# Items of 244 rows in a routed AdaLN block: fewer moving columns per product, a reordered bridge into the expert loop, a loop with a running item number

## What is computed

```python
mod = (_silu(L0_c) @ L0_wmod).reshape(4, 6, 1, -1)            # sa, ca, ga, sb, cb, gb
h = _layernorm(x) * (1 + ca) + sa
q, k, v = heads(h @ Wq.T), heads(h @ Wk.T), heads(h @ Wv.T)
q, k = _rms_norm(q), _rms_norm(k)                             # per head, width 16
y = softmax(q @ k.T * 16 ** -0.5) @ v
vn = v / norm(v)
x = x + ga * ((y - sum(y * vn) * vn) @ Wo.T)
h = _layernorm(x) * (1 + cb) + sb                             # 2048 rows
probs = softmax(h @ router_w.T)
w = _top_p_weights(probs, 0.9)                                # 2048 x 8, zero where not kept
for e in range(8):
    out += ((silu(h @ gate_w[e].T) * (h @ up_w[e].T)) @ down_w[e].T) * w[:, e:e + 1]
x = x + gb * out
```

## Time and profile before

| | |
|---|---|
| median of 3 runs | 493.86 us |
| the profiled execution | 491.9 us |
| its span, first to last instruction | 490.3 us |
| TensorE busy | 457.1 us, 93% |
| VectorE / ScalarE / GpSimd busy | 334.5 / 258.9 / 199.1 us |
| mean granted TensorE clock | 0.986 |

### The profile page before, as it was taken

How to read it: one execution, slowest core, us unless ns; L and a number is a source line. 1 busy time by engine, 2 the same in 40 slices (tenths; PEclk the granted TensorE clock), 3 DMA queues, 4 the chain that set the end, 5 groups by cost and what they waited for, 6 DMA issues and landing times. The chain is left out here.

```text
span 490.3 us, 10014 instructions
## 1 busy us (share of the span) xinstructions
PE 457.1 (93%) x3466; PEld 349.2 (71%) x3466; DVE 334.5 (68%) x790; ACT 258.9 (53%) x358; POOL 199.1 (41%) x235
## 2 busy tenths in 40 slices
PE   7978989998999999999999799999989999999992
PEld 7373343454535445345899799989979999999992
DVE  3597786499767976768898768557437585665542
ACT  3237878767776788677452245344226353524230
POOL 4142033013100200004235667566756666676755
PEclk8899999999999999999999899999999999999998
DMA  8601203901010100223334547757537556565443
GB/s 258 225 1 45 87 2 30 128 16 43 2 45 1 44 1 11 79 87 111 109 127 114 128 92 171 198 111 192 89 68 177 131 128 158 117 119 111 78 77 45
DMA packets 30785, 46.01 MB, mean 94 GB/s; under 512 B 3588, under 2 KB 22276, under 8 KB 30728
## 3 DMA queue, kind: packets, MB, share of 16 engines
q0 software_dynamic: 11936, 22.50, 25.9%
q1 hardware_dynamic: 18792, 22.77, 14.1%
HBM read 34.44 MB, written 12.93 MB: 97 GB/s over the span
## 5 line engine op out<-in xcount | busy, mean ns | idle before, releaser
L645 ACT ACTIVATE probs<-psS 128x1024 f32<-128x1024 f32 x128 | 123.1, 1028 | 21.4 <-PE psS L1487 21.1
L1730 PE MATMUL psS<-hs_hi,w_hi 128*128 128x256 f32 x400 | 113.1, 283 | 3.0 <-issue 2.3
L1730 PE MATMUL psS<-hs_lo,w_hi 128*128 128x256 f32 x400 | 112.4, 281 | 0.0
L1730 PE MATMUL psS<-hs_hi,w_lo 128*128 128x256 f32 x400 | 112.3, 281 | 0.0
L506 POOL DMA_INDIRECT out<-y_sel,idx_out x44 | 76.7, 1744 | 35.8 <-DVE y_sel L1293 22.7
L1730 PEld LDWEIGHTS psS<-hs_hi,w_hi 128*128 128x128 f32 x400 | 75.3, 188 | 4.1 <-issue 4.1
L1730 PEld LDWEIGHTS psS<-hs_lo,w_hi 128*128 128x128 f32 x400 | 75.3, 188 | 0.0
L1730 PEld LDWEIGHTS psS<-hs_hi,w_lo 128*128 128x128 f32 x400 | 75.3, 188 | 0.0
L492 POOL DMA_INDIRECT h_sel<-h_rows,idx_in x50 | 55.8, 1115 | 43.7 <-DVE sel L1259 19.3
L1594 PE MATMUL psY<-probs,v_aug 128*32 128x512 f32 x512 | 68.2, 605 | 0.0
L697 ACT ACTIVATE silu_g<-psS 128x512 f32<-128x512 f32 x50 | 29.8, 598 | 59.2 <-PE psS L1730 58.8
(11 more groups left out here) (224 smaller groups left out, 736.7 us busy)
## 6 DMA issues: line engine op xcount, KB each, us to landing
w_in<-gateT SPq DMA_DIRECT2D x8, 512.0 KB, 4.8
w_in<-upT SPq DMA_DIRECT2D x8, 512.0 KB, 4.5
w_in<-downT SPq DMA_DIRECT2D x8, 512.0 KB, 4.7
h_rows<-h_nat SPq DMA_DIRECT2D x4, 528.0 KB, 3.1
x_all<-x SPq DMA_DIRECT2D x4, 512.0 KB, 5.2
h_rows<-mod_table POOLq DMA_DIRECT2D x4, 512.0 KB, 15.0
out<-x_all SPq DMA_DIRECT2D x4, 512.0 KB, 2.9
mod_rows<-mod_table SPq DMA_DIRECT2D x3, 512.0 KB, 5.7
```

Source lines behind the costliest of these rows:

```text
L645: act.activation(probs[:, gk % 4, 2 * pair:2 * pair + 2, :], psS[:, pair, :, :], ACT.Exp, scale=ATT_SCALE).then_inc(probs_done, 1)
L1730: mm = pe.matmul(ps[:, i * SW:(i + 1) * SW], w, v[:, k, :], start=at == 0, stop=at == 3 * KC - 1)
```

## The change

- **244 rows.** An item has SW = 2 x PR rows, PR = 122. TSLOTS (tiles of an expert) becomes 18 instead of 16. Gather, scatter, transposes, `sel` and `output` work on 122 partitions; `gate_up` moves 244 columns, `downs` has 122 stationary columns and still moves 256. Tile and row of a place come from a multiplication, a rounding by adding and subtracting 1.5 * 2^23, and one fused step, all in float32, in place of shift, mask and two casts.
- **Full last items.** Since 9 items of 244 hold more than 2048 rows, code for a ninth item of an expert (`clear_places`, `replace_places`) is added behind a comparison; it runs only where an expert has nine items.
- **Bridge.** On VectorE `take_weights(3)` goes ahead of `product(2, 0)`; the second list's `rows_of_places(1)`, `count_items` and the tiles of experts 2 to 7 go later; on ScalarE `gate(3, 0)` goes between the two `round_hidden(2, ...)`; on TensorE `list_tokens(1)` goes behind the first half of `downs(2)`.
- **Loop.** The loop for a fourth and later item counts a register `item` up; it makes six turns, and for four items the body stands in the fourth.
- **Early lists.** `list_early(0)` is summed ahead of the value matmuls of step 11 and copied by itself, `list_early(1)` behind them; `turn(0)` goes from step 15 to step 14; `turn_h` of step 6 goes behind that step's value matmuls.
- **Roots.** One Newton step of three instructions and one step of higher order in four; its factor 0.375 is applied where the root is used.
- **Start and v.** The twelve `kT` matmuls and two copies are gone, `stay_awake(18)` is `stay_awake(30)`; the parts of the first two tiles of sequence 0 are copied by ScalarE, those of the other two by GpSimd as before; the copy to `v_aug` is made by ScalarE for all sequences.

```diff
+    PR = 122
+    TSLOTS = S * -(-T // (S * PR))
-    SW = S * P
+    SW = S * PR
...
+                    turns = end - a
+                    with eng.register() as item:
+                        eng.reg_mov(item, before + a)
+                        with eng.Fori(0, turns) as i:
+                            with eng.If(n > (i + turns - 3) % turns + a):
+                                m = eng.snap(item, min_val=EARLY + a, max_val=EARLY + ITEMS)
...
+                                body(e, False, m)
+                                eng.reg_add(item, item, 1)
...
-                    pool.indirect_dma_start(h_sel[:, k, :], None, h_rows[0:rows, :],
-                                            bass.IndirectOffsetOnAxis(ap=idx_in[:, k:k + 1], axis=0)).then_inc(gathered, 16)
+                    pool.indirect_dma_start(h_sel[0:PR, k, :], None, h_rows[0:rows, :],
+                                            bass.IndirectOffsetOnAxis(ap=idx_in[0:PR, k:k + 1], axis=0)).then_inc(gathered, 16)
...
+            for tt in range(2):
+                q, k = parted[:, tt, 0:H, :, :], parted[:, tt, H:HG, :, :]
+                act.wait_ge(lo_done, tt + 1 + 1)
+                act.copy(q[:, :, 1:3, :], q[:, :, 0:4:3, :]).then_inc(parts0_done, 1)
+                act.copy(k[:, :, 1, :], k[:, :, 3, :]).then_inc(parts0_done, 1)
+                act.copy(k[:, :, 2, :], k[:, :, 0, :]).then_inc(parts0_done, 1)
+            take_v(0, range(TT))
...
+                dve.tensor_tensor(t, y, y, ALU.mult).then_inc(newton_step, 1)
+                dve.tensor_tensor(t, t, z, ALU.mult).then_inc(newton_step, 1)
+                dve.scalar_tensor_tensor(out=t, in0=t, scalar=-10.0 / 3.0, in1=t, op0=ALU.add, op1=ALU.mult).then_inc(newton_step, 1)
+                dve.scalar_tensor_tensor(out=y, in0=t, scalar=5.0, in1=y, op0=ALU.add, op1=ALU.mult).then_inc(newton_step, 1)
...
-            stay_awake(18)
-
-            pe.wait_ge(awake_in, 2)
-            for cols in (P, 2 * P - 12, 2 * P):
-                for _ in range(4):
-                    pe.matmul(psS[:, 1, 1, 0:cols], kT[:, 1, 0, 0:P], kT[:, 1, 0, 0:cols], start=True, stop=True)
+            stay_awake(30)
...
-                    tok = slice(j * P, (j + 1) * P)
+                    tok = slice(j * PR, (j + 1) * PR)
...
-                list_tokens(1)
                 pe.wait_ge(w_ready, 6)
                 downs(2, 1, js=(0,))
+                list_tokens(1)
                 turn(4)
```

More of the change, by code:

```diff
@@ L58, in adaln_block @@
     RING = 4
-    SW = S * P
+    SW = S * PR
+    ROUND = 1.5 * 2.0 ** 23
     GATE_ROW, SHIFT_ROW, SCALE_ROW = 0, B, 2 * B
@@ L282, in item_counts, with last_item, walk_items @@
             return n, before
-        def walk_items(eng, body, between):
+        def last_item(e):
+            return (T - (SLOTS0 * PR if e < EXPERTS0 else 0)) // SW
+        def walk_items(eng, body, between, fullest=None):
             for e in range(E):
@@ L290, in others @@
                         with eng.If(n > i):
+                            if fullest:
+                                with eng.If(i > last_item(e) - 1):
+                                    fullest(e, before + i)
                             body(e, False, before + i)
@@ L295, in last_others @@
                     end = TSLOTS // S
[L296 to L299, removed]
+                    turns = end - a
[4 more added lines that the diff above has]
+                                m = eng.snap(item, min_val=EARLY + a, max_val=EARLY + ITEMS)
+                                if fullest:
+                                    with eng.If(m - before > last_item(e) - 1):
+                                        fullest(e, m)
+                                body(e, False, m)
+                                eng.reg_add(item, item, 1)
                 body(e, True, before)
@@ L442, in double_parts @@
                 pool.tensor_copy(k[:, :, 2, :], k[:, :, 0, :]).then_inc(parts_done, 1)
-            for tt in range(TT):
+            for tt in (2, 3):
                 double_parts(0, tt)
@@ L985, in take_logits @@
                                 psM[:, 1, 0:TT * E].rearrange("p (t e) -> p t e", e=E)).then_inc(logit_done, 1)
-            dve.wait_ge(ident_done, 1)
-            for half in range(2):
-                dve.tensor_copy(kT[:, 1, 0, half * P:(half + 1) * P], ident[:, :]).then_inc(awake_in, 1)
             dve.wait_ge(x0_in, 16)
@@ L1289, in output @@
                 for k in range(S):
-                    row = sel[:, bass.ds(m % RING, 1), k, :].rearrange("p a c -> p (a c)")
+                    row = sel[0:PR, bass.ds(m % RING, 1), k, :].rearrange("p a c -> p (a c)")
                     if last:
                         dve.wait_ge(last_ps, k + 1)
-                    weighed = dve.scalar_tensor_tensor(out=into[:, k, :], in0=down_rows(k, last),
+                    weighed = dve.scalar_tensor_tensor(out=into[0:PR, k, :], in0=down_rows(k, last),
                                                        scalar=row[:, bass.ds(e1, 1)], in1=row[:, 1 + E:], op0=ALU.mult, op1=ALU.mult)
```

213 lines of the change are left out of this document (131 added, 82 removed).

## The result

The changed kernel takes 679.57 us (median of 4 runs, 678.44 to 680.16), the kernel before 493.11 us (4 runs): a ratio of 1.3853, 95% interval 1.3807 to 1.3898. The ratios with intervals come from executions in the faster of the chip's two states alone, and differ a little from the quotient of the medians, here 1.378. I had forecast 478.5 us.

A forecast was written before the change was run, and what follows sets the result against it. TensorE, busy 457.1 of 490.3 us, was taken as the bound. Columns -7.0, bridge -3.4, loop -0.2, start -1.1, attention -1.5, last sequence -1.2 sum to -14.4: 477.5 from 491.9, given as 478.5 us, range 471.5 to 485.5.

The forecast's parts named there:

- column term: Gate and up products: 244 columns save 6.5 ns on each of 1200 matmuls, 7.8 us, less 0.8 in gather waits: -7.0.
- the gathers take the place of the columns: Rival: the chain turn, sel, gather, turn sets an item's pace, all 7.8 us become waits for h_sel, 485.5 us; chance 0.13.
- signs of being wrong: 244 columns at 118 ns, `downs` at another distance, 26 or more items, or TensorE's h_sel waits above 4 us in sum.
- Start, attention, last sequence: Before the items: cheaper roots and shared copies -1.1 at the start, -1.5 in attention; reordered last sequence -1.2 us.
- Bridge: Before item 4: the 2.56 us gather wait and low clock go, first product at 275.3 instead of 278.70: -3.4 us.
- What I called late next: Bridge: `count_items`, now between `product(3, 1)` and `split_input(4)`, with ScalarE's list copy and `round_input(4)` behind it.
- The reason given for the long gather(4): Bridge: its first instruction took 3.58 us, not 1.04, beside `w_lo` and two `a_lo`, instructions with two SBUF inputs.
- gather(5) under the big tile instructions: Bridge: by the skill's rule this gather would be long, about 2.5 us back; the prediction relied on the rows instead.
- Loop: Expert 3's fourth item: the 2.30 us issue wait falls to about 1.1, about 1.0 comes behind it: -0.2 us.
- Short stationary operands: Rival: loads of 122 columns in `downs` take twice a matmul's distance, 71 us added: 549 us; chance 0.03.

The follow-up runs named there:

- e2: Kernel before, only the gathers of items 1 and later over 122 rows instead of 128, scatters at 128: 604.39 us, ratio 1.2333.
- e3: Kernel before, only the scatters over 122 rows instead of 128, gathers at 128: 671.42 us, ratio 1.3701.
- e9: Changed kernel whole, but gathers (except the first, of 128) and scatters carry 120 rows instead of 122: 481.95 us against 490.29, ratio 0.9831.
- e10: e9 with the two moves of e8: 482.56 us, ratio 0.9841.
- e1: Changed kernel with PR = 128 (256-row items, DMAs of 128 rows), every other part kept: 486.01 us against 490.8, ratio 0.9914.
- e11: Kernel before, gate and up products moving 244 of 256 columns, nothing else: 487.93 us against 490.29, ratio 0.9932.
- e4: e1 with gate and up products moving only 244 of 256 columns: 483.93 us, ratio 0.9874.
- e8: e1 with two moves: ScalarE's round_input(4) before the counts' wait and list copy, VectorE's count_items before product(3, 1): 484.29 us against 492.08, ratio 0.9845.
- e6: Kernel with the old bridge order and 120 rows in each DMA: as quick as 128 rows, 4188 small packets; its time is not in the text.
- e7: Kernel with the old bridge order and 112 rows in each DMA: time a little above the expected 485 to 493 us.

## Why the prediction was wrong

**The step that failed** is one clause of the column term: "the way from a turn through `take_weights` and the gather to the next turn hardly does (122 instead of 128 rows in each DMA)". It took the cost of an indirect DMA as one that falls a little with its rows. No row of before showed a gather or scatter of any number but 128, so this was a cost without a row, and I neither bounded it nor asked what sets it. With 122 rows the gather instruction takes 1.7 times as long, the scatter 1.8 times, and landing 2.3 times (e2, e3, and the rows above); e9 shows that this is all of the loss. My rival "the gathers take the place of the columns" had the right place, and the wrong price: it let the gain vanish (+7 us), as it too assumed the gather of before. I bounded the waits that return at 2.5 us; they were 129. Of the signs of being wrong that the prediction names, waits for h_sel above 4 us in sum is the one that came.

**The other steps** can be read from e9. Starts on TensorE's timeline, worked out from first scores, first product of items 0, 4, 5 and 24, the first matmul of `downs(2)`, and the end:

```
stretch                                     before     e9     difference   forecast
start to first scores                        35.91    32.71     -3.2         -1.1
attention of sequences 0 to 2               146.29   144.17     -2.1         -1.5
last sequence to the first product           46.77    45.80     -1.0         -1.2
items 0 to 3, to downs(2)                    42.08    40.68     -1.4       (columns)
downs(2) to first product of item 4           7.65     6.19     -1.5         -3.4
item 4 to first product of item 5            10.13    12.88     +2.7       (columns)
items 5 to 24                               180.03   175.69     -4.3       (columns, loop)
last item to the end                         21.44    22.18     +0.7          0
sum                                         490.3    480.3     -10.0        -14.4
```

- *Start, attention, last sequence*: right in sign and nearly in size. The start scatters: the six profiles with the new start have their first scores between 32.7 and 35.6 us, 33.9 in the mean, the seven with the old one between 34.9 and 36.3, 35.8 in the mean; so its gain is about 1.9 us and not the 3.2 of this one execution. The last sequence takes 46.8 us in e10 and 47.4 in e1, so its gain is not there in every execution either.
- *Columns* (-7.0): 244 columns stand 113 ns apart as the `kT` rows had said, but 256 cost 118 and not 118.5, so each product saves 5 ns rather than 6.5, and the gross gain is 1200 x 5 = 6.0 us, the lower of my bounds. From items 5 to 24 the profiles have -4.3 (e9), -3.0 (e11) and, e4 against e1, -3.7, of 19 x 48 x 5 ns = 4.6. By medians less is left, 2.1 (e1 to e4) and 2.4 us (e11). The mechanism was right and the size off.
- *Bridge* (-3.4): the sum of the two rows is +1.3, so the step brought nothing. The first half came as forecast: in e1 gather(4) is 1.04 and 0.98 us long instead of 3.58 and 0.98, and turn(4) waits 0.21 us at most in e1, e4, e8, e9 and e10. What I called late next was mis-sized: I gave it 0.7 us (of 4.1), but the counts, the loaded value and the list copy stand ahead of the input (1.35 us of wait in e9, 2.15 in e1, 2.32 in e4), and list 1 then comes late for gather(5), so TensorE waits another 1.25 us at turn(5) in e9. With the two moves the same two rows are 17.05 (e8) and 16.70 us (e10), against 17.78 before and 19.08 in e9.
- *The reason given for the long gather(4)* does not hold by itself. e6, e7 and e11 have the old order of the bridge, with 120, 112 and 128 rows in each DMA. Gather(4) and `w_lo` lie beside each other in all of them as in the kernel before, first in e7, then in e11:

```profile
266.44 3.53 POOL L493 DMA_INDIRECT h_sel<-h_rows,idx_in  x1 [1.21 <-DVE sel L1260]
266.67 1.21 DVE L795 TENSOR_TENSOR w_lo<-w_in,w_hi 128x1024 fp32r<-128x1024 f32 x1
```

```profile
266.26 1.23 POOL L492 DMA_INDIRECT h_sel<-h_rows,idx_in  x1 [1.23 <-DVE sel L1259]
267.79 1.38 POOL L492 DMA_INDIRECT h_sel<-h_rows,idx_in  x1 [0.30 <-issue]
266.48 1.23 DVE L794 TENSOR_TENSOR w_lo<-w_in,w_hi 128x1024 fp32r<-128x1024 f32 x1
```

  `w_lo` begins 0.2 us behind the gather in each, and the instruction takes 3.53 us in e7 but 1.23 in e11 and 1.19 in e6; what makes it long in some executions stays open. So the wait of 2.56 us that the new bridge was to remove was in good part one execution's: turn(4) waits 2.23, 1.28 and 0.86 us in e7, e6 and e11, whose two rows sum to 16.76, 16.07 and 15.81 us. Against these the rebuilt bridge costs 1.6 to 3.5 us (18.38 in e1, 19.34 in e4, 19.08 in e9), and the two moves bring it back to within 0.3 to 1.0 us of them (e8 against e6 and e7, e10 against e11).
- *gather(5) under the big tile instructions*: I had set the Trainium skill's rule of the shared SBUF interfaces (GPSIMD Engine Reference, Key points) against rows that showed one slow stretch only. e9 has gather(5) at 1.04 and 1.85 us: 0.85 us back and not 2.5. Both of its instructions lie beside two-input tile instructions on VectorE, and only one is long; in e8 they take 1.22 and 1.01 us beside the same. That conflict may be part of it, but no run here parts it from other causes.
- *Loop* (-0.2): in e9 two waits for issue of 1.17 and 1.24 us against one of 2.30: +0.1. In e1 the second is 0.38.
- *Short stationary operands* (the 549 us rival): out; 122 columns are no slower to use than 128.

Without the DMA cost the gain is 8.3 us by medians (e9 against its own kernel before), for 14.4 in the sum: the forecast would have been too high by the bridge and the columns, and e9's 481.95 us would have lain inside the range.

## What to carry to other kernels

Before a tile gets another number of rows, look at every DMA that has this number as its outermost dimension: 128, 112 and 120 went alike here, 124 and 122 made each instruction 1.3 to 1.8 times as long, and 122 more than doubled the time to landing. A cost that no row of the profile shows needs a bound as wide as what is unknown, above all on an engine (GpSimd at 64%) whose queue the whole loop passes. And after a wait is removed, read the order on the engine that delivers the next operand; here two moved lines brought back most of what the rebuilt bridge had lost. And a wait that is to be removed should be looked for in more than one execution: the 2.56 us of the one profile were 0.86 to 2.23 in three others of the same order.

## What the runs showed that I had not expected

- An indirect DMA of 122 rows brings seven packets of 8 B for each packet of data (42,700 for 6100 scattered rows in e3), of 124 rows three, of 112 rows none, of 120 rows 12 for a whole gather.
- A slow scatter delays a quick gather behind it: e3 lost more than e2, 181 against 114 us, by waits for gathers of 128 rows (108.9 us).
- The weight loads, which SyncE issues, landed later too: the gate weights after 6.8 us instead of 4.8, the up weights after 7.3 instead of 4.5.
- Executions of one kernel on one chip spread with the granted clock: those of e11 from a span of 482.1 us at 0.992 to 487.6 at 0.984. The two executions of the kernel before at 0.992 span 488.5 and 488.7, the three of e11 482.1 to 484.3. Over all executions of both kernels, a fit with one slope against the clock gives 3.9 us for the columns alone at equal clock (an estimate, give or take 0.6), more than the 2.4 of the medians. But waits lower the clock, and e11 has more of them, so this part need not be free of what the columns cost elsewhere; why e11 was more often at the lower clock stays open.
